# In a layer's last step, two of four probability tiles reach the context product through DRAM instead of through TensorE transposes

## The reference

```python
for i in (1, 2):
    h = layer_norm(x, ln_scale, ln_offset)
    q, k, v = h @ wq + bq, ctx @ wk + bk, ctx @ wv + bv      # 16 heads of 128
    k, v = concat(k, bias_k), concat(v, bias_v)              # one learned key and value per head
    w = softmax(q @ k.T / sqrt(128))
    x = x + (w @ v) @ wo + bo
x = x + gelu(layer_norm(x) @ w_fc1 + b_fc1) @ w_fc2 + b_fc2
```

## Time and profile before

| what | us |
|---|---|
| median of 3 runs | 494.83 |
| the 3 runs | 494.57, 496.68, 494.83 |
| the profiled execution's own time | 495.07 |
| its span | 493.2 |
| PE busy | 487.6 (99% of the span) |
| POOL, DVE, ACT busy | 410.8, 391.1, 331.9 |

### The profile page before, as it was taken

One profiled execution on the slowest core, in us unless ns is written; L12 is line 12 of the kernel. 1 busy time (PEld: TensorE's weight loads), 2 busy tenths in 40 slices (PEclk: granted clock), 3 DMA queues, 4 the chain that ended last, 5 costly groups with the idle time before them and its releaser, 6 DMA issues.

```text
span 493.2 us, 11022 instructions
## 1 busy us (share of the span) xinstructions
PE 487.6 (99%) x3216; PEld 443.0 (90%) x3216; DVE 391.1 (79%) x917; ACT 331.9 (67%) x728; POOL 410.8 (83%) x378
## 2 busy tenths in 40 slices
PE   8999999999999999999999999999999999999997
PEld 7789899989999898999988889989989999999997
DVE  4988878878877878856789778778788888767796
ACT  5777767666766857665486777758666677758541
POOL 4877999989898998996597979989989898999561
PEclk9999999999999999999999999999999999999999
DMA  6536876756566686702115785676866566660011
GB/s 240 182 108 206 286 213 191 229 179 192 187 202 181 213 215 189 214 23 66 43 44 169 241 252 178 207 210 189 235 184 194 194 190 186 194 179 2 3 42 44
DMA packets 53159, 82.56 MB, mean 167 GB/s; under 512 B 5904, under 2 KB 33936, under 8 KB 53136
## 3 DMA queue, kind: packets, MB, share of 16 engines
q1 hardware_dynamic: 53136, 82.28, 54.3%
HBM read 53.42 MB, written 28.84 MB: 167 GB/s over the span
## 4 chain that ended last, share of the span: by engine, by line
PE 94%; DMA 2%; DVE 1%; issue 1%; SPq 1%; ACT 1%; POOL 0%; ACTq 0%; POOLq 0%
PE ring L1226 69%; PE ps_ctx L1226 10%; PE acc L1226 10%; DMA spill<-blocks 1%; PE ring L1272 1%; PE ring L1297 1%; DMA wf_lo<-spill 1%; SPq L287 1%; DVE pT_lo L921 0%; PE ring L1309 0%; PE acc L1303 0%; ACT q_hi L597 0%; DVE blocks L899 0%; PE ps_ctx L1309 0%; PE acc L1329 0%
## 5 line engine op out<-in xcount | busy, mean ns | idle before, releaser
L936 DVE TENSOR_REDUCE row_max<-ring 128x1 f32<-128x512 f32 x112 | 76.2, 688 | 28.0 <-PE ring L1226 27.6
L660 ACT ACTIVATE probs<-ring,shift 128x512 f32<-128x512 f32 x112 | 76.5, 683 | 18.9 <-DVE shift L941 18.6
L430 POOL TENSOR_TENSOR v_lo<-v_sum,v_hi 128x512 fp32r<-128x512 f32 x64 | 82.9, 1297 | 2.7 <-ACT v_hi L610 2.7
L899 DVE STREAM_TRANSPOSE blocks<-probs 128x512 f32<-128x512 f32 x108 | 70.1, 687 | 4.7 <-POOL probs L437 4.3
L437 POOL TENSOR_SCALAR probs<-probs,inv 128x512 f32<-128x512 f32 x80 | 55.6, 703 | 21.6 <-DVE inv L949 21.6
L442 POOL TENSOR_TENSOR pT_lo<-wf_lo,pT_hi 128x1024 fp32r<-128x1024 f32 x28 | 67.1, 2418 | 0.2 <-ACT pT_hi L627 0.2
L1226 PE MATMUL ring<-pT_lo,v_hi 128*128 128x256 f32 x208 | 58.5, 281 | 0.6 <-ACT probs L660 0.4
L592 ACT ACTIVATE k_hi<-ring,cols 128x512 fp32r<-128x512 f32 x57 | 37.8, 689 | 31.3 <-PE ring L1226 31.2
L1226 PE MATMUL ring<-pT_hi,v_lo 128*128 128x256 f32 x208 | 58.0, 279 | 0.0
L1226 PE MATMUL ring<-pT_hi,v_hi 128*128 128x256 f32 x208 | 58.0, 279 | 0.0
L1226 PE MATMUL ring<-wv_lo,cT_hi 128*128 128x256 f32 x200 | 55.9, 280 | 0.0
(11 more groups left out here) (216 smaller groups left out, 1633.8 us busy)
## 6 DMA issues: line engine op xcount, KB each, us to landing
spill<-blocks SPq DMA_DIRECT2D x54, 512.0 KB, 2.9
wf_lo<-spill SPq DMA_DIRECT2D x112, 128.0 KB, 3.3
wf_hi<-spill SPq DMA_DIRECT2D x104, 128.0 KB, 3.1
wk_raw<-wk_in SPq DMA_DIRECT2D x17, 256.0 KB, 2.7
wq_raw<-wq_in SPq DMA_DIRECT2D x17, 256.0 KB, 3.6
wv_raw<-wv_in SPq DMA_DIRECT2D x16, 256.0 KB, 3.8
vrows<-vrows_in SPq DMA_DIRECT2D x16, 256.0 KB, 4.0
wo_raw<-wo_in SPq DMA_DIRECT2D x16, 256.0 KB, 2.6
```

What stands on the lines that cost most here:

```text
L430: pool.tensor_tensor(v_lo[:, 2 * m:2 * m + 2, :], v_sum[:, m % 2, :].rearrange("p (t c) -> p t c", c=PW), v_hi[:, 2 * m:2 * m + 2, :].bitc ...
L660: act.activation(probs[:, u, q, :], ring[S_BANKS[where][QTB * u + q]][:], ACT.Exp, bias=shift[:, u, q:q + 1], scale=SCALE, accum_out=row_s ...
L899: last = dve.transpose(blocks[:, u % 2, :, :, q, :].rearrange("p g c b -> p c g b"), probs[:, u, q, :].rearrange("p (c g b) -> p c g b", g ...
L936: dve.reduce_max(row_max[:, u, q:q + 1], ring[S_BANKS[where][QTB * u + q]][:], AX_X).then_inc(max_done, 1)
```

## The change

Only the last step of each layer changes. Units 0 and 1 of the pair take the way of `step`: blocks transposed on DVE, written to DRAM, read back, rounded by `round_moved` on ACT, rests made by `moved_rest` on DVE. Units 2 and 3 keep `transpose_own` (now 4 tiles, not 8). Around it the orders on the engines change: the own tiles 0 to 3 disappear from PE's, ACT's and DVE's lists; POOL scales unit 0 at the front, ahead of `moved_rest`, and both `residual` calls go behind the weights; ACT scales unit 1 and unit 3 earlier and rounds the moved tiles ahead of the last value rounding; DVE makes `inverse_sums(0)` and `(1)` and the two block transposes ahead of the maxima of units 2 and 3. SP loads `wo` first, then writes and reads two units, then loads `wk`. The remaining edits only change the numbers that semaphores are compared with.

```diff
 SP   def last_step(pair, layer, final=False):
+    sp.wait_ge(wo_split, pair); load_wo(pair)
+    for u in range(2): write_blocks(pair, layer, u, False)
+    for u in range(2): read_blocks(pair, layer, u, False)
+    for u in range(2, NU):
+        sp.wait_ge(landed[u], QB * LOAD * pair)
+        sp.sem_inc(blocks_ready, 1); sp.sem_inc(landed[u], QB * LOAD); sp.sem_inc(spilled[u], LOAD)
     if not final: wait wk_split, load_wk(pair + 2)
-    sp.wait_ge(wo_split, pair); load_wo(pair)
 POOL def last_step
     split_wo(pair - 1)
-    residual(layer, 0)
-    normalise(pair, 0, [0])
+    normalise(pair, 0, [0, 1])
+    normalise(pair, 1, [1])
     moved_rest(pair - 1, layer, 2)
     value_rest(pair, 0)
     moved_rest(pair - 1, layer, 3)
-    normalise(pair, 0, [1])
-    normalise(pair, 1, [1])
+    normalise(pair, 2, [0, 1])
     value_rest(pair, 1)
     split_wk(pair + 1)                 # behind a wait for k_filled
-    normalise(pair, 2, [0, 1])
-    residual(layer, 1)
+    residual(layer, 0)
+    value_rest(pair, 2)
     split_wo(pair)                     # behind a wait for outputs_done
-    value_rest(pair, 2)
     value_rest(pair, 3)
+    residual(layer, 1)
 ACT  def last_step
     exponential(pair, 1, 1)
+    normalise(pair, 1, [0])
     round_v(pair, 0); round_moved(pair - 1, 3); round_o(pair - 1, 1)
     exponential(pair, 2, 0); round_v(pair, 1); exponential(pair, 2, 1)
-    normalise(pair, 1, [0])
     round_o(pair - 1, 2); exponential(pair, 3, 0)
+    exponential(pair, 3, 1); normalise(pair, 3, [0, 1])
     round_o(pair - 1, 3)
-    round_own 0, 1, 2; exponential(pair, 3, 1)
     round_v(pair, 2)
-    round_own 3; normalise(pair, 3, [0])
+    round_moved(pair, 0); round_moved(pair, 1); round_v(pair, 3)
     round_k(pair + 1, 0) or, in the final layer, the load of the Gelu table
-    round_v(pair, 3); normalise(pair, 3, [1])
     round_o(pair, 0); round_o(pair, 1)
-    round_own 4, 5, 6, 7
+    round_own 0, 1, 2, 3               # units 2 and 3
 DVE  def last_step
     maximum(pair, 1, 0)
-    split_o(pair - 1, 0)
     shifts(pair, 1, 0); maximum(pair, 1, 1)
+    shifts(pair, 1, 1); inverse_sums(pair, 0); split_o(pair - 1, 0)
     sum_v(pair, 0)
-    inverse_sums(pair, 0); shifts(pair, 1, 1)
+    inverse_sums(pair, 1); transpose_blocks(0); transpose_blocks(1); sum_v(pair, 1)
     maximum and shifts of units 2 and 3, split_o(pair - 1, 1) between them
+    inverse_sums(pair, 2); split_o(pair - 1, 2); inverse_sums(pair, 3); sum_v(pair, 2)
-    split_own 0, 1; inverse_sums(pair, 2)
     split_o(pair - 1, 3)
-    split_own 2; inverse_sums(pair, 3); sum_v(pair, 3); split_own 3
+    moved_rest(pair, 0); sum_v(pair, 3); moved_rest(pair, 1)
 PE   def last_step
     context(3, "last")
-    transpose_own 0, 1, 2, 3 (with waits for p_ready_pool, p_ready_act, exp_done)
     unit_output(1)
+    wait exp_done of scores (2, 1)
     project_v(3, "last"); unit_output(2)
     if not final: wait wk_split, project_k(0)
     unit_output(3)                     # raises outputs_done
-    wait own_split
+    wait pT_split[0]
     context(0, "own")
-    wait own_split
+    wait pT_split[1]
     context(1, "own")
```

More of the change, by code:

```diff
@@ L37 @@
 NS = NU * QTB
-NT = NU * 2
+NT = 4
 NK = 2 * BATCH
@@ L271, in write_blocks @@
             def write_blocks(pair, layer, u, first):
-                done = pair - layer
                 if not first or layer > 0:
-                    hold(landed[u], QB * LOAD * done)
-                hold(blocks_ready, NU * done + u + 1)
+                    hold(landed[u], QB * LOAD * pair)
+                hold(blocks_ready, NU * pair + u + 1)
                 sp.dma_start(spill[u].rearrange("p g r -> p (g r)"),
@@ L280, in read_blocks @@
             def read_blocks(pair, layer, u, first):
-                done = pair - layer
                 if not first or layer > 0:
-                    hold(pT_split[u], done)
-                hold(spilled[u], LOAD * (done + 1))
+                    hold(pT_split[u], pair)
+                hold(spilled[u], LOAD * (pair + 1))
                 for g in range(QB):
@@ L321, in step, with last_step @@
                     load_wv(pair + 2)
-            def last_step(pair, final=False):
+            def last_step(pair, layer, final=False):
+                sp.wait_ge(wo_split, pair)
+                load_wo(pair)
+                for u in range(2):
+                    write_blocks(pair, layer, u, False)
+                for u in range(2):
+                    read_blocks(pair, layer, u, False)
+                for u in range(2, NU):
+                    sp.wait_ge(landed[u], QB * LOAD * pair)
+                    sp.sem_inc(blocks_ready, 1)
+                    sp.sem_inc(landed[u], QB * LOAD)
+                    sp.sem_inc(spilled[u], LOAD)
                 if not final:
@@ L619, in round_moved @@
             def round_moved(pair, layer, u, first=False):
-                act.wait_ge(landed[u], QB * LOAD * (pair - layer + 1))
+                act.wait_ge(landed[u], QB * LOAD * (pair + 1))
                 if u < 2:
@@ L655, in exponential @@
                 act.wait_ge(shift_ready, NS * pair + QTB * u + q + 1)
-                if not first:
-                    act.wait_ge(blocks_ready, NU * (pair - 1 - layer) + u + 1)
+                if not first or layer > 0:
+                    act.wait_ge(blocks_ready, NU * (pair - 1) + u + 1)
                 if q == QTB - 1:
@@ L783, in last_step @@
                 exponential(pair, 2, 1, "last", layer)
-                normalise(pair, 1, [0])
                 round_o(pair - 1, 2, "last")
                 exponential(pair, 3, 0, "last", layer)
+                exponential(pair, 3, 1, "last", layer)
+                normalise(pair, 3, [0, 1])
                 round_o(pair - 1, 3, "last")
[L788 to L791, removed]
                 round_v(pair, 2, layer)
-                round_own(pair, layer, 3)
-                normalise(pair, 3, [0])
+                round_moved(pair, layer, 0)
+                round_moved(pair, layer, 1)
+                round_v(pair, 3, layer)
+                if final:
+                    act.activation(table_load[:], dim_cols[:, 0:1], ACT.Gelu)
                 if not final:
                     round_k(pair + 1, 0, "last")
[L797 to L800, removed]
                 round_o(pair, 0, "own")
                 round_o(pair, 1, "own")
[L803 to L806, removed]
+                for j in range(NT):
+                    round_own(pair, layer, j)
                 if not final:
@@ L1120, in last_step @@
                 maximum(pair, 1, 0, "last")
-                split_o(pair - 1, 0, "last")
                 shifts(pair, 1, 0)
                 maximum(pair, 1, 1, "last")
+                shifts(pair, 1, 1)
+                inverse_sums(pair, 0)
+                split_o(pair - 1, 0, "last")
                 dve.wait_ge(wv_split, pair + 1)
                 sum_v(pair, 0, "last")
-                inverse_sums(pair, 0)
-                shifts(pair, 1, 1)
+                inverse_sums(pair, 1)
+                transpose_blocks(pair, layer, 0)
+                transpose_blocks(pair, layer, 1)
+                sum_v(pair, 1, "last")
                 maximum(pair, 2, 0, "last")
-                sum_v(pair, 1, "last")
                 shifts(pair, 2, 0)
@@ L1132, in last_step @@
                 shifts(pair, 2, 1)
-                inverse_sums(pair, 1)
                 split_o(pair - 1, 1, "last")
@@ L1479, in last_step @@
             def last_step(pair, layer, final=False):
-                done, own = pair - layer, NT * layer
                 pe.wait_ge(k_split, NK * pair + 1)
```

116 lines of the change are left out of this document (52 added, 64 removed).

## The result

| | before | after | ratio, 95% interval |
|---|---|---|---|
| median, 22 runs each | 495.19 us | 496.83 us | 1.0033 [1.0024, 1.0043] |
| the same kernels on another chip (30 and 7 runs) | 495.13 us | 496.75 us | 1.0043 [1.0028, 1.0057] |

The change costs 1.64 us, 0.3%. The forecast was 495.9 from a before of 494.83: a loss of 1.1. The profiled execution of the kernel after took 496.79 us with a span of 495.0.

The account below looks back on a forecast made before the run. PE, busy 99% of the span, was taken as the bound, with POOL's lateness deciding; -0.07 in layer 0 and +1.2 in layer 1 made +1.1 on 494.83, so 495.9 us, range 493.2 to 497.2.

Parts of the forecast that it names:

- PE spared: Last step of each layer: 16 transposes fewer on PE, 1.66 us a layer, 3.3 us in two, bounding the time at 491.5.
- Holds: Last steps: each DVE moved_rest keeps POOL out for 0.98 us, so the residual pair takes some 3.4 instead of 1.44.
- Rival (a): Last steps: POOL is not held by DVE's moved rests; layer 0 gains 1.0, layer 1 0.3, time 493.6; chance 0.22.
- rival (b): Last steps: PE waits for nobody, so the whole saving shows, time 491.5; chance 0.05.
- Rival (c): Last steps: DVE's block transposes hold POOL too, costing 1.9 us a layer, 3.8 in all, time 499.7; chance 0.05.
- PE's waits: Last steps: PE waits for POOL 0.65 and 0.9 in layer 0; for DVE 1.1 and 0.3, POOL 1.6 in layer 1.
- Gain and loss by layer: unit_output(0) of the last step: 0.07 us earlier in layer 0, 1.26 later in layer 1, carried as 1.2.
- Rival (d): Last steps: POOL's chain is later than counted, deciding at 0.7 us per layer, time 497.3; chance 0.06 beyond 0.5%.
- Transfers: Last steps: writes and reads of both units take 8.9 us, hidden by ACT's own list, costing nothing; ACT waits for no DMA.
- The forecast's two terms: Last steps: a gain of 0.07 us in layer 0 and a loss of 1.2 in layer 1, together +1.1.

Follow-up runs that it names:

- after, again: The kernel after, unchanged, run a second time beside other variants on the same chip; 496.75 us.
- e2b: Kernel after with DVE's two moved rests of both last steps replaced by two block transposes each; 494.67 us against 495.13 before, ratio 0.9993.
- e1: Kernel after with POOL's residual(layer, 0) moved behind split_wo; 495.13 us against 495.52 before, ratio 0.9996.
- e4: Kernel after with 16 satisfied semaphore waits (8 instructions) in PE's list ahead of the warm-up; 499.6 us against 495.52 before, ratio 1.0080.
- e3: Kernel after with residual(layer, 0) behind split_wo and split_wk ahead of value_rest(1); 494.98 us against 495.52 before, ratio 0.9988.
- e6: Kernel after with both weight splits earlier on POOL and 64 satisfied waits ahead of layer 0's last-step scores; 494.14 us against 495.13 before, ratio 0.9981.
- e5: Kernel after with 64 satisfied waits (32 instructions) spread ahead of layer 0's last-step scores; 496.53 us against 495.13 before, ratio 1.0028.

## Why the prediction was right, and where it was not

- **PE spared.** 3.3 us forecast from 16 transposes a layer; PE's busy time fell by 2.3 by the page and by 2.9 in after, again, with 32 transposes fewer; part of the rest is that matmuls behind a wait show longer (0.39 and 0.50 for 0.28 and 0.39).
- **Holds.** Forecast 0.98 each, on `residual(0)`: the pair took 3.45 against the forecast 3.4, and `wo_lo` ended at 230.38 against 230.3. e2b shows the cause, e1 that the hold falls on whatever POOL runs at the time. Rival (a) had it that there are no holds; what the time is without them is now known: 494.67 and not (a)'s 493.6; 0.7 of that is the place of the instructions, which (a) lacked too. In rival (b) PE waits for nobody; in both last steps it waits for POOL 2.4 us in all. Rival (c) is out by POOL's 2.12 us for three scalings and 2.43 for the moved rest beside DVE's four transposes: ordinary durations (0.70 and 2.42 in the earlier trace rows).
- **PE's waits.** Layer 0: forecast 0.65 and 0.9, measured 0.46 and 0.62 (PE came 0.3 and 0.4 later than forecast, POOL 0.1). Layer 1: 1.1, 0.3 and 1.6, measured 0.93, 0.2 and 1.26. Gain and loss by layer, 0.07 and 1.2, came out as 0.15 to 0.2 and 1.1 to 1.2. Rival (d) did not happen.
- **Transfers.** Forecast: ACT waits for no DMA. It did, 0.35 in layer 0 and 0.41 in layer 1. This step failed. In layer 0 SP issued the eight reads in 5.15 us, not 4.0: one of them, at 218.35, took 1.91, and the packet of instructions beside it ran from 218.30 to 219.88. But in layer 1 it issued them in 3.68 (445.95 to 449.63), and ACT waited all the same, so why the reads landed that late stays open. Both waits are for unit 1, and ACT's rounding still ended (224.84 and 454.82) before DVE was through with the sum ahead of `moved_rest(1)`, which started at 225.38 and 455.31, so they cost nothing.
- **What was missing.** A term for where the instructions lie. Taking 16 transposes out of layer 0 moved a place of PE's code from inside layer 1's loop to 8 instructions behind its exit. That gave 0.75 and cost 1.42: +0.7. With it the sum is -0.2 + 1.1 - 0.75 + 1.42 = +1.6, and 1.64 was measured. The forecast's two terms, -0.07 and +1.2, were right for the reason given; what it lacked came to no more than 0.7 because its two parts have opposite signs, and that was luck: with 8 instructions more ahead of the place (e4) the change costs 2.3 us more.
- **What could have been better** is one line of POOL's order: `residual(0)` feeds only the end of the layer and stood ahead of the weight that PE waits for. Moving it is worth 1.8 us by the ratios, about the change's whole cost. With that the change is about level with before, and with `split_wk` earlier as well it is slightly ahead.

Open: in layer 0's first two loop passes e1, e3, e4 and e6 lost 0.4 to 0.9 us by their profiles (56.1 to 56.5 against 55.7), the other profiles nothing. In e1, e4 and e6 an SP issue of 1.23 to 1.34 beside a packet of instructions (at 40.45 to 40.76) stands there, where the other profiles have 0.36; in e3 nothing of the kind, and e1 and e3 have their PE code in the same place as after. How the gap's length depends on its place was seen at three distances only, one profile each but for the middle one.

## What to carry to other kernels

Before work is moved from the bottleneck to another engine, ask what form the new instructions have: here each DVE instruction with two SBUF inputs kept GpSimd out for about 1 us, and the price fell on whatever stood in GpSimd's list then. Put that list in the order in which the bottleneck needs its results; a sum that only the end needs does not belong ahead of a weight. And where a kernel loops, taking some instructions out ahead of a loop can move the time by a microsecond either way at its exit or in its first pass: look there for a wait on issue and for a stretched DMA issue, and for a packet of instructions in the trace, before you credit or blame the edit, and repeat with a few idle instructions added.

## What the runs showed of the hardware

- PE stood still for 1.10 to 2.15 us at one fixed place of its instructions, 8 instructions earlier in the work for 8 instructions added, 12 later for 12 removed; inside the loop it cost no PE gap but a stretched SP issue (1.29 to 1.61 for 0.43) and late reads (1.2 us in e5), 0.6 to 1.2 us in all, in the first pass only.
- An SP issue that met a 16 KiB packet of instructions ended 0.36 to 0.38 us behind the packet's end, in all 31 issues of over 1.2 us; PE went on 1.22 to 1.55 us behind it.
- In e4 an idle time of 2.15 us was followed by a granted clock of 0.50 (0.86 on the mean over 433 to 445); the clock stayed at 1.00 behind those of up to 1.70.
- Which POOL instruction pays for the hold is decided at its boundaries: DVE's instruction, issued while POOL's ran, got in ahead of POOL's next one: of the residual pair at 223.74 in the kernel after (3.45 for 1.44), of the value rest at 224.06 in e1 (2.29 for 1.28).
- Float32 block transposes on DVE held nothing up: beside them POOL's three scalings took 2.12, its moved rest 2.43, its residual pair 1.45.
